# A perceiver layer on one core: the end of the second attention, with the last projections, the row norms and TensorE's filler matmuls rearranged

## The chip, the cores and the metric

The kernel runs on one core of a Trainium2 chip. The metric is the device time of one execution in microseconds (us). The engines are TensorE (PE; its weight loads are PEld), VectorE (DVE), ScalarE (ACT), GpSimd (POOL) and SyncE (SP), which issues most DMAs. Each runs its own instruction list in order; they wait for each other by semaphores, so an instruction behind a waiting one waits too.

## The reference, cut to what matters

```python
x = x + cross_attention(layernorm(x), ctx_768, ...)   # 16 heads, 4096 keys for each of 4 batches
x = x + attention(layernorm(x), w_qkv, ..., w_out)    # window of 32 tokens on either side, 16 heads
x = x + experts(layernorm(x), Wr, br, W1, b1, W2, b2) # 16 banks, 2 picked for each token

def experts(t, ...):
    probs = softmax(t @ Wr + br)                      # the router
    topv, topi = top_k(probs, 2)
    ...                                               # gate-weighted sum of the picked banks
```

x is 4 batches of 256 tokens of 256 numbers, in fp32. The change touches the end of the second line and the beginning of the third.

## The kernel before, in words

The 1024 tokens are held as 8 tiles of 128 rows, two for each batch. The first attention takes the first 900 us or so. The second works in 16 pairs (`PAIRS`) of a batch and a group of four heads. For pair i TensorE computes masked scores for the row maxima (`max2`, L799 and L805), which VectorE reduces (L1564) and splits into three bf16 pieces; TensorE turns these (`neg2`, L814), ScalarE copies them out (L1347), TensorE computes the transposed scores with the maximum subtracted (`scores2`, L833, L839 and L846), ScalarE takes the exponential in two halves (L1340), and TensorE multiplies by the values (`weigh2`, L863). In its list the steps of neighbouring pairs are interleaved. ScalarE copies a pair's output to `o_raw2` (L1299).

Outputs of the first 14 pairs (`WIDE`) go through small DMAs (`close_up`, and `close_rest` on ScalarE's queue) that put heads side by side in `o_close2` and sums in `total2`. VectorE takes the reciprocal (`inverse_two`, L1589); GpSimd multiplies (L2165) and adds the value bias (L2167), in `norm_two(u)`, u from 0 to 6. Pairs 14 and 15, the second half of the last batch's heads, go another way: TensorE turns them to tokens (`turn_out`, L872), VectorE divides (`tokens`, L1596 and L1600), TensorE turns them back (`turn_back`, L879), and ScalarE adds the bias (`out_back`, L1369).

The output projection of batch 2 is `project_third(0)` and `(1)` (L897), that of batch 3 is `project_wide` (L915, the half from u = 6) and `project_turned` (L922, the half that was turned back). VectorE adds them to x (`add_third`, L1609; `add_last2`, L1631) and computes the third layer norm: statistics (L1460, L1463), an inverse square root by small steps (L1472 to L1490). Normalised rows `xn3` are made on three engines: tiles 0 to 3 on GpSimd (L2177), 4 and 5 on ScalarE (`rows3`, L1376), 6 and 7 on VectorE (`apply`, L1499). TensorE transposes them (`turn3(b)`, L1010), ScalarE copies them out (L1382), TensorE computes the router's logits (L1029, 16 columns wide), and VectorE picks two banks a token (`choose`). TensorE then counts the tokens of each bank (`counts`, L1085); VectorE makes from it the list of tokens of each expert tile, on which the gathers and the loads of weights depend. The expert stage follows until the end.

`keep_busy(n, bank)` (L1017) multiplies the bf16 identity by itself n times, into a PSUM bank that nothing reads at that time. The "constants" of the change are these.

The order of work is written out by hand: each engine's block is its list. GpSimd, ScalarE and VectorE take their parts in an order of their own that has to fit TensorE's.

Of the kernel before, what the change touches and what calls it, by code (L numbers as in the profile page):

```python
# [12 lines left out]
ACT = mybir.ActivationFunctionType  # L13
# [4 lines left out]
BATCH, SEQ, EMB = 4, 256, 256  # L18
# [245 lines left out]
def build(nc, a, out, scratch):  # L264
    ctx = ExitStack()
    with ctx:
# [295 lines left out]
        def _(e):  # L562
# [348 lines left out]
            def project_wide():  # L911

                e.wait_ge(pool_norm2, WIDE // 2)
# [4 lines left out]
            def project_turned():  # L918

                e.wait_ge(act_ocopy2, PAIRS + 1)  # L920
# [77 lines left out]
            def turn3(b):  # L998
# [4 lines left out]
                else:  # L1003
                    if b == 2:
                        e.wait_ge(act_rows, TT)
                    else:
                        e.wait_ge(dve_rows3, BT)
# [50 lines left out]
            project_third(0)  # L1058
# [3 lines left out]
            turn_out(PAIRS - 2)  # L1062
            project_third(1)
            weigh2(PAIRS - 1, 0)
            weigh2(PAIRS - 1, 1)
            turn_out(PAIRS - 1)
            project_wide()
            turn_back()
            project_turned()
            turn3(0)  # L1070
            turn3(1)
            logits(range(0, 2), 2)
            keep_busy(8, 5)
            turn3(2)
            turn3(3)
            keep_busy(6, 5)
            logits(range(2, 3), 3)
            logits(range(3, 4), 4)
# [142 lines left out]
        def _(e):  # L1221
# [142 lines left out]

            def out_back():
# [6 lines left out]
            def rows3():  # L1372

                e.wait_ge(dve_root3, 2)
                for i in upper[:BT]:
                    e.activation(xn3[:, i], x[:, i], ACT.Identity, scale=rstd[:, i:i + 1], bias=sq[:, i:i + 1]).then_inc(act_rows, 1)  # L1376
# [3 lines left out]
            def turned3(b):  # L1380
                e.wait_ge(pe_t3, b + 1)
# [32 lines left out]
            ocopy2(PAIRS - 1)  # L1414
            out_back()
            turned3(0)
            turned3(1)
            rows3()
            turned3(2)
            turned3(3)  # L1420
# [33 lines left out]
        def _(e):  # L1454
# [319 lines left out]
            add_third(0)  # L1774
            inverse_two(WIDE // 2 - 1)
            tokens(0)
            add_third(1)
            e.wait_ge(dve_third, BT)
            statistics(upper[:BT])
            tokens(1)  # L1780
# [5 lines left out]
            shifted = slice(upper[0], upper[BT])  # L1786
            e.scalar_tensor_tensor(sq[:, shifted], mv[:, shifted, 0], -1.0, rstd[:, shifted], ALU.mult, ALU.mult).then_inc(dve_root3, 1)
            apply(xn3, upper[BT:], dve_rows3)
# [211 lines left out]
        def _(e):  # L2000
# [160 lines left out]
            def norm_two(u):  # L2161
# [3 lines left out]
                e.tensor_tensor(o, o, inverse2, ALU.mult).then_inc(pool_omul2, 1)  # L2165
                e.wait_ge(pool_omul2, u + 1)
                e.tensor_scalar_add(o, o, bv2[:, u % KE:u % KE + 1]).then_inc(pool_norm2, 1)  # L2167

            for u in range(WIDE // 2):
# [4 lines left out]
                if u == KE * (BATCH - 1) - 2:  # L2174
                    e.wait_ge(dve_root3, 1)
                    for i in range(TT // 2):
# [55 lines left out]
        def _(e):  # L2232
# [141 lines left out]
            for part in range(2):  # L2374
# [3 lines left out]
                else:  # L2378
                    e.wait_ge(act_rows, TT)
                    e.wait_ge(dve_rows3, BT)  # L2380
# [130 lines left out]
```

## Time and profile before

| | us |
|---|---|
| median of 3 runs | 1181.17 |
| lowest and highest of them | 1180.66, 1182.34 |
| the profiled execution | 1179.86 |
| its span, first to last instruction | 1178.1 |
| pair 15's maximum pieces done on VectorE | 935.2 |
| the last x rows added (L1631) | 947.5 to 948.4 |
| counts of banks read by VectorE | 961.8 |
| first expert tile turned (L1131) | 983.0 |

Times within the span are counted from its first instruction. TensorE is busy in 98% of the span, and the granted clock is 0.987 of full speed on the mean: full speed is 2.4 GHz, and its other level is 1.2 GHz. The profiled execution is 1.31 us faster than the median of the others. The rest of this text is about some 30 us in the last fifth of the span, between 930 and 962 us.

### The profile page before, as it was taken

The numbers are of one execution on the slowest core, as the hardware profiler recorded it, in microseconds if no ns is written. First come the engines' busy times: TensorE is split into PE (matmuls) and PEld (weight loads), VectorE is DVE, ScalarE is ACT, GpSimd is POOL, SyncE is SP. The second block draws the span as 40 slices with busy tenths as digits, with TensorE's granted clock in tenths as the row PEclk, the third lists the DMA queues.
The fourth block names the chain that finished last, engine by engine and source line by source line (L and its number), as shares of the span: only waits on it lengthen the run. The fifth ranks groups of instructions, "written<-read, shape, count | busy, mean of one in ns | idle before, by whom it ended". The sixth has DMA issues, their size and how long they took to land.

```text
span 1178.1 us, 29516 instructions
## 1 busy us (share of the span) xinstructions
PE 1150.7 (98%) x12028; PEld 712.7 (60%) x12028; DVE 841.1 (71%) x1637; ACT 706.0 (60%) x897; POOL 362.5 (31%) x336
## 2 busy tenths in 40 slices
PE   8989999999999999999999999999999989999998
PEld 5455555566555566654556654444556578877777
DVE  5987899977899987789997789982365672333234
ACT  4447788877788877778887778886333310211120
POOL 3386663113631513534311240021211312222220
PEclk9999999999999999999999999999999988999999
DMA  7766766555575465656654445401310119999993
GB/s 241 116 153 184 181 136 151 124 123 129 128 181 127 102 139 140 153 123 131 152 123 97 102 100 124 82 17 36 91 30 18 38 45 399 414 404 401 395 377 117
DMA packets 64654, 186.26 MB, mean 158 GB/s; under 512 B 20104, under 2 KB 29960, under 8 KB 56584
## 3 DMA queue, kind: packets, MB, share of 16 engines
q1 hardware_dynamic: 60260, 172.70, 53.3%
q0 software_dynamic: 2432, 7.11, 1.8%
q10 hardware_dynamic: 1828, 4.57, 1.1%
q8 instruction: 95, 1.56, 0.6%
q14 instruction: 39, 0.32, 0.1%
HBM read 137.60 MB, written 39.58 MB: 150 GB/s over the span
## 4 chain that ended last, share of the span: by engine, by line
PE 91%; DVE 3%; ACT 3%; issue 1%; POOL 1%; DMA 1%; SPq 0%; ACTq 0%; DVEq 0%; POOLq 0%
PE psum L750 22%; PE psum L732 17%; PE psum L702 11%; PE psum L1160 5%; PE psum L1188 5%; PE psum L600 5%; PE psum L616 4%; PE psum L805 2%; PE psum L1185 2%; PE psum L1154 2%; DVE part_max L1525 1%; ACT wts L1250 1%; PE psum L933 1%; PE psum L799 1%; PE psum L839 1%; PE psum L583 1%
## 5 line engine op out<-in xcount | busy, mean ns | idle before, releaser
L1535 DVE TENSOR_REDUCE part_max<-psum 128x1 f32<-128x512 f32 x952 | 599.6, 686 | 88.9 <-PE psum L702 87.1
L1250 ACT ACTIVATE wts<-psum 128x1024 f32<-128x1024 f32 x512 | 518.9, 1025 | 100.8 <-PE psum L732 100.0
L750 PE MATMUL psum<-wts,vals 128*17 128x256 f32 x4096 | 307.2, 384 | 0.5 <-ACT o_raw L1293 0.5
L732 PEld LDWEIGHTS psum<-queries,keys 51*128 51x128 f32 x2048 | 155.9, 185 | 187.3 <-issue 154.1
L732 PE MATMUL psum<-queries,keys 51*128 51x256 f32 x2048 | 255.2, 326 | 2.2 <-ACT queries L1282 0.2
L702 PE MATMUL psum<-keys,queries 51*128 51x512 f32 x1024 | 218.5, 409 | 4.2 <-DVE part_max L1525 2.5
L750 PEld LDWEIGHTS psum<-wts,vals 128*17 128x17 f32 x4096 | 74.9, 95 | 119.1 <-issue 93.4
L2013 POOL CAST key_high<-key_low 128x1024 fp32r<-128x1024 f32 x28 | 29.1, 1038 | 355.1 <-ACT key_low L1263 355.1
L702 PEld LDWEIGHTS psum<-keys,queries 51*128 51x128 f32 x1024 | 109.7, 185 | 20.1 <-DVE part_max L1525 10.7
L1441 ACT ACTIVATE hid<-psum,b1s 128x128 f32<-128x128 f32 (+1 forms) x124 | 31.7, 351 | 114.6 <-PE psum L1160 78.2
L2015 POOL TENSOR_TENSOR key_low<-key_low,key_high 128x1024 fp32r<-128x1024 f32 x28 | 66.6, 2379 | 2.3
L1160 PE MATMUL psum<-xTt,w1s 128*128 128x128 f32 x544 | 63.6, 275 | 0.4 <-issue 0.4
L1935 DVE TENSOR_SCALAR hid<-psum,b1s 128x128 f32<-128x128 f32 (+1 forms) x124 | 30.5, 314 | 45.5 <-PE psum L1160 42.4
L1160 PEld LDWEIGHTS psum<-xTt,w1s 128*128 128x128 f32 x544 | 62.2, 192 | 0.7 <-issue 0.6
L1188 PE MATMUL psum<-w2s,hid 128*128 128x256 f32 x272 | 62.1, 382 | 0.0
L2215 POOL DMA_INDIRECT rows_y<-yout,to_row x22 | 21.8, 990 | 129.6 <-DVE yout L1944 129.6
L1188 PEld LDWEIGHTS psum<-w2s,hid 128*128 128x128 f32 x272 | 50.4, 190 | 11.9 <-issue 5.7
L2028 POOL TENSOR_TENSOR ctx_lo<-ctx_in,ctx_hi 128x1536 fp32r<-128x1536 f32 x16 | 55.7, 3480 | 1.3
L1269 ACT ACTIVATE vals<-psum 128x512 f32<-128x512 f32 x64 | 38.3, 600 | 28.5 <-PE psum L616 16.4
L1263 ACT ACTIVATE key_low<-psum,bk_two 128x1024 f32<-128x1024 f32 x28 | 31.2, 1116 | 36.3 <-PE psum L600 36.3
L1564 DVE TENSOR_REDUCE neg_max<-psum 128x4 f32<-128x640 f32 x32 | 26.4, 825 | 33.6 <-PE psum L805 33.6
L1944 DVE COPY yout<-psum 128x256 f32<-128x256 f32 x22 | 9.3, 425 | 56.7 <-PE psum L1188 39.3
(277 smaller groups left out, 1387.7 us busy)
## 6 DMA issues: line engine op xcount, KB each, us to landing
w1s<-in_W SPq DMA_DIRECT2D x31, 1024.0 KB
w2s<-in_W SPq DMA_DIRECT2D x31, 1024.0 KB
keys<-k_high SPq DMA_DIRECT2D x232, 128.0 KB, 4.1
keys<-k_low SPq DMA_DIRECT2D x116, 128.0 KB, 4.6
k_high<-key_high SPq DMA_DIRECT2D x28, 512.0 KB, 5.1
k_low<-key_low SPq DMA_DIRECT2D x28, 512.0 KB, 5.5
ctx_in<-in_ctxT SPq DMA_DIRECT2D x12, 768.0 KB, 7.6
ctx_in<-in_ctxT ACTq DMA_DIRECT2D x4, 768.0 KB, 12.4
```

The lines of the kernel that those rows point to most:

```text
L600: t = e.matmul(bank(first + odd), w[rows, r, hp * P:(hp + 1) * P], c[rows, p, r * CH:(r + 1) * CH], start=(r == 0 and n == 0), stop=(r == ...
L616: m = e.matmul(bank(first + odd)[:, 0:EMB], c[rows, p, at:at + P], w[rows, r], start=(r == 0 and n == 0), stop=(r == CB - 1 and n == 2))
L702: e.matmul(bank(LEAD_BANKS[m % 2] + i if m < LEAD else M_BANKS[(2 * m + i) % 3]), queries[g % 3][64 * i:64 * i + STK, hh, qt * P:(qt + 1) ...
L732: m = e.matmul(bank(S_BANKS[S_NO["s", n] % 2] + i)[:, hh * SEQ:(hh + 1) * SEQ], keys[64 * i:64 * i + STK, hh, c, at:at + P], queries[g % 3 ...
L750: i = e.matmul(bank(O_BANK)[32 * j:32 * j + VW, 0:SEQ], vals[:, t, h * VW:(h + 1) * VW], wts[n % NW][:, j * SEQ:(j + 1) * SEQ], start=(t = ...
L1160: i = e.matmul(dst[:, q * P:(q + 1) * P], w1s[w[0]][:, k, hc * P:(hc + 1) * P], xTt[j % 2][:, k], start=(k == 0), stop=(k == KE - 1))
L1188: i = e.matmul(dst, hid[j % 2][:, hc], w2s[w[0]][:, hc], start=(hc == 0), stop=(hc == HC - 1))
L1250: i = e.activation(wts[n % NW], s_bank(job, 2), ACT.Exp, scale=QSCALE)
L1269: i = e.activation(vals_of[:, t:last + 1:CH // P, :, 0:HD], s_bank(job, 2).rearrange("p (t h w) -> p t h w", t=2, w=HD)[:, :, 0:HEADS], AC ...
L1535: e.reduce_max(part_max[g % 2][:, hq, c:c + 1], bank(M_BANKS[n % 3]), AX_X).then_inc(dve_max, 1)
L2015: e.tensor_tensor(key_low, key_f, key_high.bitcast(F32), ALU.subtract).then_inc(split_low, 1)
L2028: e.tensor_tensor(ctx_lo[:, p], ctx_in[:, p], ctx_hi[:, p].bitcast(F32), ALU.subtract).then_inc(pool_lo, 1)
```

## The change

- TensorE's `project_third(0)` stands behind `scores2(15)` and `turn_out(14)`, next to `project_third(1)`, and no longer ahead of `weigh2(14)`.
- `turn3(0)` and `turn3(1)` stand ahead of `turn_back`, and `project_wide` behind it.
- GpSimd normalises tiles 0 and 1 behind u = 4 and tiles 2 and 3 behind u = 5, where it did four behind u = 4. The last bias of u = 6 is added by ScalarE (`bias_wide`), and `project_wide` waits for that.
- VectorE takes its last `inverse_two` and `tokens(0)` ahead of `add_third(0)`, and `tokens(1)` ahead of the statistics of tiles 4 and 5.
- Of tiles 4 to 7, ScalarE normalises one (4) and VectorE three (6, 7, 5 in this order); batch 3 is turned and its logits are computed ahead of batch 2.
- Six filler matmuls are added ahead of `turn_out(15)`, and the eight behind the first logits are 26.

```diff
@@ def project_wide
-                e.wait_ge(pool_norm2, WIDE // 2)
+                e.wait_ge(act_ocopy2, PAIRS + 1)
@@ def project_turned
-                e.wait_ge(act_ocopy2, PAIRS + 1)
+                e.wait_ge(act_ocopy2, PAIRS + 2)
@@ def turn3
                     if b == 2:
-                        e.wait_ge(act_rows, TT)
+                        e.wait_ge(act_rows, TT - 1)
+                        e.wait_ge(dve_rows3, BT + 1)
@@ TensorE's list
             neg2(PAIRS - 1)
-            project_third(0)
             weigh2(PAIRS - 2, 0)
             weigh2(PAIRS - 2, 1)
             scores2(PAIRS - 1)
             turn_out(PAIRS - 2)
+            project_third(0)
             project_third(1)
             weigh2(PAIRS - 1, 0)
             weigh2(PAIRS - 1, 1)
+            keep_busy(6, L3_BANKS[1])
             turn_out(PAIRS - 1)
-            project_wide()
-            turn_back()
-            project_turned()
             turn3(0)
             turn3(1)
+            turn_back()
+            project_wide()
+            project_turned()
             logits(range(0, 2), 2)
-            keep_busy(8, 5)
+            keep_busy(26, T3_BANKS[1])
+            turn3(3)
             turn3(2)
-            turn3(3)
-            keep_busy(6, 5)
-            logits(range(2, 3), 3)
-            logits(range(3, 4), 4)
+            keep_busy(6, T3_BANKS[0])
+            logits(range(3, 4), 3)
+            logits(range(2, 3), 4)
@@ ScalarE
+            def bias_wide():
+
+                o = o_close2[(BATCH - 1) % 2][:, 0]
+                e.wait_ge(pool_omul2, WIDE // 2)
+                e.activation(o, o, ACT.Identity, bias=bv2[:, 0:1]).then_inc(act_ocopy2, 1)
+
@@ def rows3, now row3
-                for i in upper[:BT]:
-                    e.activation(xn3[:, i], x[:, i], ACT.Identity, scale=rstd[:, i:i + 1], bias=sq[:, i:i + 1]).then_inc(act_rows, 1)
+                i = upper[0]
+                e.activation(xn3[:, i], x[:, i], ACT.Identity, scale=rstd[:, i:i + 1], bias=sq[:, i:i + 1]).then_inc(act_rows, 1)
@@ ScalarE's list
             ocopy2(PAIRS - 1)
+            bias_wide()
+            turned3(0, 1)
             out_back()
-            turned3(0)
-            turned3(1)
-            rows3()
-            turned3(2)
-            turned3(3)
+            turned3(1, 2)
+            row3()
+            turned3(3, 3)
+            turned3(2, 4)
@@ VectorE's list
-            add_third(0)
             inverse_two(WIDE // 2 - 1)
             tokens(0)
+            add_third(0)
             add_third(1)
+            tokens(1)
             e.wait_ge(dve_third, BT)
             statistics(upper[:BT])
-            tokens(1)
             add_last2()
...
-            shifted = slice(upper[0], upper[BT])
+            shifted = slice(upper[0], upper[1])
...
-            apply(xn3, upper[BT:], dve_rows3)
+            apply(xn3, (upper[BT], upper[BT + 1], upper[1]), dve_rows3)
@@ GpSimd, norm_two and behind it
+                if u == WIDE // 2 - 1:
+                    return
...
-                if u == KE * (BATCH - 1) - 2:
+                if u in (KE * (BATCH - 1) - 2, KE * (BATCH - 1) - 1):
                     e.wait_ge(dve_root3, 1)
-                    for i in range(TT // 2):
+                    half = (u - KE * (BATCH - 1) + 2) * BT
+                    for i in range(half, half + BT):
@@ SyncE, store of the second half of xn3
-                    e.wait_ge(act_rows, TT)
-                    e.wait_ge(dve_rows3, BT)
+                    e.wait_ge(act_rows, TT - BT + 1)
+                    e.wait_ge(dve_rows3, BT + 1)
```

TensorE's list from the last pair's scores on (a line of before with -, of after with +; L1017 before and L1018 after are the filler matmuls; `o_close2_0_164` holds batch 2, `o_close2_1_165` batch 3, `wT0_150` to `wT3_153` the weights of pairs 14 and 15; the lines of after lie up to nine further down):

```order
 L846 MATMUL psum<-neg_rows2_0_148,ones2_141 128x160 x8
 L814 MATMUL psum<-identb_51,neg_parts2_1_147 128x128 x2
-L897 MATMUL psum<-wo2_143,o_close2_0_164 128x256 x2
 L863 MATMUL psum<-wT0_150,vals2_137 17x160 x4
 L863 MATMUL psum<-wT1_151,vals2_137 17x64 x4
```

and further down, from the turning of pair 14's output:

```order
 L872 MATMUL psum<-identf_50,o_raw2_0_154 128x128 x2
-L897 MATMUL psum<-wo2_143,o_close2_0_164 128x256 x2
+L897 MATMUL psum<-wo2_143,o_close2_0_164 128x256 x4
 L863 MATMUL psum<-wT2_152,vals2_137 17x160 x4
 L863 MATMUL psum<-wT3_153,vals2_137 17x64 x4
 L863 MATMUL psum<-wT3_153,vals2_137 17x96 x4
+L1018 MATMUL psum<-identb_51 128x128 x6
 L872 MATMUL psum<-identf_50,o_raw2_2_156 128x128 x2
+L1011 MATMUL psum<-identf_50,xn3_101 128x128 x8
+L879 MATMUL psum<-identf_50,by_tok_157 128x128 x2
 L915 MATMUL psum<-wo2_143,o_close2_1_165 128x256 x2
-L879 MATMUL psum<-identf_50,by_tok_157 128x128 x2
```

The first two matmuls of batch 2's projection have gone from ahead of pair 14's weighing to the place of the other two, behind the turning of pair 14's output. Eight transposes of normalised rows now stand ahead of the turning back, and `project_wide` behind it.

On GpSimd, around the two norms of batch 2's second half (`o_close_0_164` is batch 2, `xn_101` the normalised rows), before:

```order
L2177 TENSOR_SCALAR xn_101<-x,mv,rstd 128x256 [waits dve_root3]
L2177 TENSOR_SCALAR xn_101<-x,mv,rstd 128x256 x3
L2165 TENSOR_TENSOR o_close_0_164<-o_close_0_164,inverse_168 128x256 [waits dve_rec2]
L2167 TENSOR_SCALAR o_close_0_164<-o_close_0_164,bv_134 128x256 [waits pool_omul2]
L2165 TENSOR_TENSOR o_close_1_165<-o_close_1_165,inverse_168 128x256 [waits dve_rec2]
L2167 TENSOR_SCALAR o_close_1_165<-o_close_1_165,bv_134 128x256 [waits pool_omul2]
```

and after:

```order
L2189 TENSOR_SCALAR xn_101<-x,mv,rstd 128x256 [waits dve_root3]
L2189 TENSOR_SCALAR xn_101<-x,mv,rstd 128x256
L2174 TENSOR_TENSOR o_close_0_164<-o_close_0_164,inverse_168 128x256 [waits dve_rec2]
L2178 TENSOR_SCALAR o_close_0_164<-o_close_0_164,bv_134 128x256 [waits pool_omul2]
L2189 TENSOR_SCALAR xn_101<-x,mv,rstd 128x256 [waits dve_root3]
L2189 TENSOR_SCALAR xn_101<-x,mv,rstd 128x256
L2174 TENSOR_TENSOR o_close_1_165<-o_close_1_165,inverse_168 128x256 [waits dve_rec2]
```

Two of the four tiles have moved behind batch 2's last norm, and the last bias is gone from this engine.

## Rows read from the trace of the kernel before

**Rows 1.** The page: span, and TensorE's share of it.
```profile
span 1178.1 us, 29516 instructions
PE 1150.7 (98%) x12028; PEld 712.7 (60%) x12028; DVE 841.1 (71%) x1637; ACT 706.0 (60%) x897; POOL 362.5 (31%) x336
```

**Rows 2.** Windows of 2 us: length, busy us of engines, PEclk, DMA share, GB/s.
```profile
936.00:938.00 2.00, 0.83 (x4) 0.68 (x4) 0.00 (x0) 0.39 (x2) 1.01 (x2) 1.00 0.64 262
938.00:940.00 2.00, 2.00 (x29) 1.00 (x28) 1.54 (x2) 0.38 (x1) 0.00 (x0) 0.53 0.00 0
...
950.00:952.00 2.00, 1.84 (x21) 1.67 (x20) 1.76 (x10) 0.49 (x1) 0.00 (x0) 0.94 0.00 0
952.00:954.00 2.00, 1.34 (x7) 1.35 (x8) 1.79 (x16) 0.80 (x3) 0.00 (x0) 0.50 0.29 119
```

**Rows 3.** Timeline: start, length, engine, line, count, [idle before <-releaser]; pair 15's scores.
```profile
930.53 4.86 POOL L2177 TENSOR_SCALAR xn<-x,mv,rstd 128x256 f32<-128x256 f32 x4 [0.72 <-DVE rstd L1490]
...
933.16 0.72 PE L833 MATMUL psum<-wmaskb,identb 128*128 128x320 bf16 x4
...
933.81 0.82 PE L839 MATMUL psum<-q,k 32*128 32x160 f32 x16
...
934.81 1.30 ACT L1340 ACTIVATE wT<-psum 128x640 f32<-128x640 f32 x2 [2.67 <-PE psum L846]
...
935.36 0.72 POOL L2165 TENSOR_TENSOR o_close<-o_close,inverse 128x256 f32<-128x256 f32 x1
...
937.17 1.18 PE L897 MATMUL psum<-wo,o_close 128*128 128x256 f32 x4 [1.64 <-POOL o_close L2167]
...
938.28 1.27 PE L863 MATMUL psum<-wT,vals 128*17 128x160 f32 x24
...
938.80 1.74 DVE L1589 RECIPROCAL inverse<-total 128x256 f32<-128x256 f32 x1
...
939.48 1.25 PE L833 MATMUL psum<-wmaskb,identb 128*128 128x320 bf16 x4
...
940.66 1.23 PE L839 MATMUL psum<-q,k 32*128 32x160 f32 x16
```

**Rows 4.** Timeline from the last projections to the router's second logits.
```profile
942.23 1.03 PE L897 MATMUL psum<-wo,o_close 128*128 128x256 f32 x4
...
943.19 0.74 PE L863 MATMUL psum<-wT,vals 128*17 128x160 f32 x24
...
944.43 0.44 PE L872 MATMUL psum<-identf,o_raw 128*128 128x128 f32 x2 [0.51 <-ACT o_raw L1299]
...
946.69 1.13 PE L922 MATMUL psum<-wo,o_close 128*128 128x256 f32 x4 [0.56 <-ACT o_close L1369]
...
947.50 0.86 DVE L1631 TENSOR_TENSOR x<-psum,x 128x256 f32<-128x256 f32 x2 [1.86 <-PE psum L922]
947.66 1.04 PE L1010 MATMUL psum<-identf,xn 128*128 128x128 f32 x8
...
949.43 1.96 PE L1029 MATMUL psum<-wr,xT 128*128 128x16 f32 x16 [0.74 <-ACT xT L1382]
...
951.39 0.73 DVE L1499 TENSOR_SCALAR xn<-x,mv,rstd 128x256 f32<-128x256 f32 x2
951.51 1.09 ACT L1376 ACTIVATE xn<-x,sq,rstd 128x256 f32<-128x256 f32 x2 [2.13 <-DVE sq L1787]
...
952.65 1.97 PE L1010 MATMUL psum<-identf,xn 128*128 128x128 f32 x8 [0.81 <-ACT xn L1376]
...
955.05 3.54 PE L1029 MATMUL psum<-wr,xT 128*128 128x16 f32 x16
```

**Rows 5.** Timeline of the count of picked banks.
```profile
958.54 3.15 PE L1017 MATMUL psum<-identb 128*128 128x128 bf16 x28
...
960.92 0.23 DVE L1741 TENSOR_TENSOR both<-hots 128x64 bf16<-128x64 f32 x1
...
962.09 2.39 PE L1017 MATMUL psum<-identb 128*128 128x128 bf16 x40
```

More of the change, by code:

```diff
@@ L1370, in out_back, with row3, turned3 @@
                              bias=bv2[:, 1:2]).then_inc(act_ocopy2, 1)
-            def rows3():
+            def row3():
+                i = upper[0]
                 e.wait_ge(dve_root3, 2)
-                for i in upper[:BT]:
-                    e.activation(xn3[:, i], x[:, i], ACT.Identity, scale=rstd[:, i:i + 1], bias=sq[:, i:i + 1]).then_inc(act_rows, 1)
+                e.activation(xn3[:, i], x[:, i], ACT.Identity, scale=rstd[:, i:i + 1], bias=sq[:, i:i + 1]).then_inc(act_rows, 1)
             upper = range(TT // 2, TT)
-            def turned3(b):
-                e.wait_ge(pe_t3, b + 1)
+            def turned3(b, n):
+                e.wait_ge(pe_t3, n)
                 e.activation(xT3[b].rearrange("p k t -> p (k t)"), bank(T3_BANKS[b]), ACT.Copy).then_inc(act_t3, 1)
```

## The prediction

> **What bounds the kernel now.** The first view is the page: TensorE is busy in 98% of a span of 1178.1 us [rows 1]. A share of busy time does not tell whether a stretch is dense, so the second view is the windows: TensorE's count and time in each 2 us, and the clock that it was granted [rows 2]. The third is the timeline between 930 and 962 us [rows 3, 4, 5]. Three things are to be seen.
>
> First, a wait. Pair 14's weights were ready at 934.81 + 1.30 = 936.11, but TensorE's list had batch 2's first projection ahead of weighing them. That projection waited 1.64 us for GpSimd, whose norm began at 935.36 only, behind four normalised tiles of 4.86 us from 930.53 [rows 3]. Second, the clock. In the window with the wait, TensorE worked 0.83 of 2 us, and in the next one its clock stood at 0.53 of full, which is the 1.2 GHz level nearly throughout [rows 2]. The same instructions show the price: 1.25 us against 0.72 for the mask, 1.23 against 0.82 for the scores, 1.27 against 0.74 for the weighing [rows 3, 4]. Third, from 947.5 on a chain goes through VectorE (adds, statistics, inverse root), then the rows, eight transposes, the second logits, `choose` and the counts. Around 951.8 the clock falls again, after a window in which TensorE was busy 1.84 of 2 us, and the transposes take 1.97 us against 1.04, the logits 3.54 against 1.96, the 28 fillers 3.15 where 40 take 2.39 later [rows 2, 4, 5]. All that the experts wait for hangs on this chain.
>
> **The change part by part.** Times in the new order are estimates from the rows' starts and lengths.
>
> *Front.* The second half of pair 14's weighing starts at 936.16 and ends near 936.7. Pair 15's scores take 1.65 us (933.16 to 934.81, where the exponential begins), so they end at 938.3. In before they end near 942.05 (940.66 + 1.23, and the last of the subtraction). That is 3.7 us: 1.64 wait, 1.18 projection, 1.47 slow clock (0.53 + 0.41 + 0.53), less 0.6 now waited for the exponential.
>
> Is the projection's input there at 938.7, when the list comes to it? GpSimd now does two tiles (2.43 us, half of 4.86) from 930.53 to 933.0; the reciprocal of u = 5 ended at 933.3; multiplication and bias take 937.12 - 935.36 = 1.8 us: ready at 935.1. Hidden, with 3.5 us to spare. Tiles 2 and 3 end at 937.6 and are turned after 942: hidden. The store of these rows leaves 2.2 us later and is read by gathers 35 us on: nothing.
>
> What comes back: turning pair 14 (0.4, as pair 15's 0.44 [rows 4]), batch 2's two projections (0.9 each, 942.23 to 943.19 from start to start, where only one stood here), pair 15's weighing (0.74). Its end is 941.2, against 943.9: 2.7 us are left. Six fillers at 0.06 (2.39/40 [rows 5]) take 0.36 us inside the 0.51 that TensorE waited for ScalarE's copy: free. Pair 15 is turned by 942.1.
>
> *Middle.* From the end of the turning (944.87) to `project_turned` (946.69) lie 1.8 us in before: the division on VectorE, the turning back (0.4) and ScalarE's copy (0.5, as a tile of rows at 1.09/2), so about 0.8 for the division with its hand-overs [rows 4]. It ends at 942.8, but the turning back now stands behind eight transposes of 1.04 us, so it starts at 943.1: 0.3 us given away. It ends at 943.5, ScalarE's copy at 944.05, under `project_wide` (0.9, until 944.4). In before `project_turned` began at 946.69; now at 944.4. It is 2.3 us earlier, and so are the adds to x (947.50) and VectorE's chain. The statistics of batch 2 stand between: the same kind with the inverse root took 3.0 us (948.36 to 951.39), so alone they take at most half and fit between 942.8 and 945.2. ScalarE's new bias (nearest row 0.55) has from 941.6 to 943.5. `project_wide` waits for it: the reciprocal for it began at 938.80 in before, behind an add to x, so its small DMAs had landed by then; even at 938.8 reciprocal, product and bias are 1.74 + 0.75 + 0.5 = 3.0 us and end at 941.9, so nothing waits. From below this could be earlier than 938.8; it would gain nothing.
>
> *Row norms.* The rows began at 951.39 on VectorE, and the transposes at 952.65, when ScalarE's second tile was done: 1.26 us. Now VectorE's first two tiles are done after 0.73 us and start four transposes; its third ends after 1.10, ScalarE's one after 0.7, both before these transposes end. 0.45 us less.
>
> *Sum with the second fall of the clock as it was:* 2.3 + 0.45 = 2.75 us.
>
> *The second pause.* First logits end near 947.2, and 26 fillers at 0.06 last until 948.75; rows come at 949.9. In before the pause was 0.8 us after eight fillers. Cost at full clock: none. At half clock a filler takes 0.1125 (3.15/28), so 26 take 2.9 us; this is used in the rivals. What they may bring is a held clock: 0.93 on the transposes, 0.27 on six fillers, 1.58 on the logits (3.54 - 1.96), and of the 28 fillers, which now end the wait for the counts (958.54 + 3.15 = 961.69, while VectorE's `both` was ready at 961.15), 0.5: 3.3 us at most, from none. I take the low end. The row nearest is the window before the fall at 951.8: busy with 16-column matmuls and eight fillers, and it fell. In the new order the narrow logits, an idle us and narrow logits again still stand on both sides of the fillers, which thicken a part of it only.
>
> The Trainium skill (TensorE: Matmul & The Clock Gate, "HAM oscillation") puts the loss of the clock down to long idle gaps between groups of matmuls. By that rule this trace should not have lost it around 951.8, where TensorE had been busy 1.84 of 2 us; it did, so the measured row decides here. By the rule the new order would keep the full clock and come out at the time of the first rival below.
>
> **Own time and the median.** The profiled execution took 1179.86, 1.76 over its span; the median is 1181.17. Less 2.75 these are 1177.1 and 1178.4. The expert stage starts with the list that this chain makes, its loads of weights too, so all of it shifts; I forecast 1178.4 us against the median.
>
> **The rivals.**
> *Held clock* (22%): the 3.3 us above come on top: 6.0 us less, 1175.1. For it: 28 fillers at half clock brought it back at 962 [rows 5]. Against it: narrow logits on both sides. A part of it, for instance only the last logits at full clock, lies between.
> *The front saves less* (20%): the slow spell at 938 to 941.5 is in this execution, and nothing shows that it is in those of the median. Without it 1.47 us of the 2.75 were never lost there: 1.3 us less, 1179.9, which is within 0.2% of before.
> *Half clock through the fillers* (6%), the slower side: between 934.8 and 936.2 TensorE still waits for pair 15's last maxima and for the exponential, and if the clock falls at about 941 all the same, the new denser stretch pays the 1.5 us, the first logits pay 1.58, and 26 fillers last 2.9 instead of 1.55. `project_turned` begins at 945.9, logits end at 950.3, fillers at 953.2, against 952.65 for the transposes of before: +0.6 us, 1181.8, and 1182.5 if the weighing pays too. It decides from the point where these three exceed the 2.75 us gained.
> *The change does not do what it says* (2%): the DMAs or the turned projections take a new wait somewhere and the counts come when they came, 1181.2.
>
> **How the numbers follow.** The forecast itself has 50%, with its own range 1177.4 to 1179.4. A difference under 0.2% (2.4 us) can't be told from none here; the forecast of 2.75 is close to it, and I give 29 of its 50 to faster and 21 to the same. Held clock gives 22 to faster, the smaller front 19 to the same and 1 to faster, the slower case 3 to slower and 3 to the same, the last 1 to the same and 1 to slower. Faster 0.52, same 0.44, slower 0.04. The range runs from a partly held clock, 1175.6, to the smaller front and some scatter of the median, 1180.8.
>
> **What would show it.** In the trace after: pair 14's weighing straight behind the exponential, without a wait for GpSimd; pair 15's scores over by 938.3, and at 0.72 and 0.82 us for mask and scores; x added from 945.2; the first four transposes of the last batches at 949.9; the 26 fillers at 1.55 us. The clock between 949 and 957 tells the forecast from the held clock: transposes at 0.5 us for four, logits at 1.0 for eight. Wrong would be a fall before 945, a turning back that waits for VectorE, or a `project_wide` that waits for ScalarE's bias.

## The result, and the profile after

| | before | after |
|---|---|---|
| median, of 8 runs each on one chip | 1181.85 | 1173.72 |
| lowest and highest | 1180.54, 1182.78 | 1172.78, 1178.00 |
| the profiled execution | 1179.86 | 1173.59 |
| its span | 1178.1 | 1171.8 |
| mean granted clock in it | 0.987 | 0.994 |

The medians differ by 8.1 us, and their quotient is 0.9931. The ratio given with the runs is 0.9945, with a 95% interval of 0.9925 to 0.9965, which is 4 to 9 us: the changed kernel is faster, by less certain an amount than the medians alone suggest. The forecast was 1178.4, with a range down to 1175.6, so it was wrong. What came is the first rival, the held clock (1175.1), with a little more gained in order. The range had left that rival's own time out, although it had a chance of 22%.

The page of the profile after, against [rows 1]: TensorE has 24 more instructions and is busy 5.8 us less.

```profile
span 1171.8 us, 29565 instructions
PE 1144.9 (98%) x12052; PEld 709.0 (61%) x12052; DVE 841.8 (72%) x1638; ACT 705.4 (60%) x897; POOL 361.7 (31%) x335
```

The windows of 2 us after: length, busy us (count) of TensorE, its weight loads, VectorE, ScalarE and GpSimd, the granted clock, then the DMAs. The clock stands at 1.00 where [rows 2] have 0.53, 0.94 and 0.50, although TensorE is idle for 0.6 us in two windows.

```profile
936.00:938.00 2.00, 2.00 (x38) 1.48 (x32) 1.37 (x1) 0.70 (x2) 1.63 (x2) 1.00 0.03 14
938.00:940.00 2.00, 2.00 (x21) 1.48 (x23) 1.14 (x5) 0.98 (x2) 0.36 (x4) 1.00 0.60 248
...
946.00:948.00 2.00, 1.37 (x25) 1.19 (x22) 1.69 (x12) 0.09 (x1) 0.00 (x0) 1.00 0.00 0
948.00:950.00 2.00, 1.43 (x15) 1.33 (x15) 1.90 (x14) 1.24 (x3) 0.00 (x0) 1.00 0.14 59
950.00:952.00 2.00, 2.00 (x24) 2.00 (x25) 1.22 (x8) 0.35 (x1) 0.00 (x0) 1.00 0.50 203
952.00:954.00 2.00, 1.55 (x28) 1.37 (x25) 1.79 (x16) 0.00 (x0) 0.00 (x0) 1.00 0.03 8
```

TensorE's timeline after, in place of [rows 3] and [rows 4]: start, length, engine, line, tiles, count, and in brackets the wait ahead of it.

```profile
935.12 0.97 PE L863 MATMUL psum<-wT,vals 128*17 128x160 f32 x24
936.03 0.72 PE L833 MATMUL psum<-wmaskb,identb 128*128 128x320 bf16 x4
936.68 0.83 PE L839 MATMUL psum<-q,k 32*128 32x160 f32 x16
...
937.85 1.89 PE L897 MATMUL psum<-wo,o_close 128*128 128x256 f32 x8
939.67 0.74 PE L863 MATMUL psum<-wT,vals 128*17 128x160 f32 x24
940.35 0.51 PE L1018 MATMUL psum<-identb 128*128 128x128 bf16 x6
...
942.07 0.42 PE L879 MATMUL psum<-identf,by_tok 128*128 128x128 f32 x2
942.33 1.03 PE L915 MATMUL psum<-wo,o_close 128*128 128x256 f32 x4
943.19 1.03 PE L922 MATMUL psum<-wo,o_close 128*128 128x256 f32 x4
944.05 1.85 PE L1030 MATMUL psum<-wr,xT 128*128 128x16 f32 x16
945.76 1.61 PE L1018 MATMUL psum<-identb 128*128 128x128 bf16 x26
948.57 1.09 PE L1011 MATMUL psum<-identf,xn 128*128 128x128 f32 x8 [1.21 <-DVE xn L1508]
949.50 0.50 PE L1018 MATMUL psum<-identb 128*128 128x128 bf16 x6
949.91 1.96 PE L1030 MATMUL psum<-wr,xT 128*128 128x16 f32 x16
951.72 0.24 PE L1087 MATMUL psum<-both,ones 128*128 128x16 bf16 x4
951.82 1.72 PE L1018 MATMUL psum<-identb 128*128 128x128 bf16 x28
```

The mask and scores of pair 15 take 0.72 and 0.83 us, not 1.25 and 1.23. The wait of 1.64 us for GpSimd is gone. The second transposes take 1.09 us against 1.97, the second logits 1.96 against 3.54, the 28 fillers 1.72 against 3.15. And there is still a wait of 1.21 us behind the 26 fillers, in which the clock does not fall.

VectorE and ScalarE on the same chain:

```profile
943.89 0.86 DVE L1640 TENSOR_TENSOR x<-psum,x 128x256 f32<-128x256 f32 x2 [0.69 <-PE psum L922]
947.79 1.05 DVE L1508 TENSOR_SCALAR xn<-x,mv,rstd 128x256 f32<-128x256 f32 x3
947.91 0.60 ACT L1384 ACTIVATE xn<-x,sq,rstd 128x256 f32<-128x256 f32 x1 [4.42 <-DVE sq L1796]
```

To compare kernels I cut this chain at five instructions: VectorE's last maximum pieces of pair 15; the first of the last x rows added (L1640 after, L1631 before); the first of the last rows normalised; their first transpose; the table `filled`, made from the counts. What lies ahead of the first does not count, and that matters, since the stretch began between 932.9 and 942.1 us in the kernels profiled below.

| profiled | pieces to x | x to rows | to transposes | to `filled` | sum |
|---|---|---|---|---|---|
| before | 12.50 | 3.89 | 1.27 | 9.16 | 26.83 |
| after | 9.44 | 3.90 | 0.78 | 6.20 | 20.32 |
| difference | 3.06 | 0 | 0.49 | 2.96 | 6.51 |

From `filled` to the first expert turn it takes 21.26 us after and 21.20 before. Then 0.7 is given back at the first split expert tile, one whose rows belong to two banks. TensorE idles 0.97 us ahead of it against 0.25 in the kernel before. Its list waits there for the tile's weights; the profile names no releaser, so that they are the cause is an inference:

```profile
989.31 3.23 PE L1156 MATMUL psum<-w1s,xTt 128*64 128x512 f32 x14 [0.97 <-issue]
```

A difference of 0.53 us already stands ahead of the change: the mask of pair 14 (L833) begins at 932.62 and not 933.16. So the spans should differ by 0.53 + 6.51 - 0.06 - 0.72 = 6.26, and they differ by 6.3. The 0.72 belongs to this execution and not to the change: in two more profiles of the same kernel (after_again and after_third below) the same wait is 0.21 and 0.42. From `filled` to the last instruction it takes 217.0 us in this profile, 216.3 and 216.4 in those two, and 216.2 in the kernel before.

### The profile page after: what moved, and what is told of

It reads as the page before. It is cut to its first block, busy times and chain, and to the rows that moved or that the text cites. A ratio compares the mean times of both kernels' runs of the same rounds, so it can differ in the third digit from the quotient of the medians.

```text
span 1171.8 us, 29565 instructions
## 1 busy us (share of the span) xinstructions
PE 1144.9 (98%) x12052; PEld 709.0 (61%) x12052; DVE 841.8 (72%) x1638; ACT 705.4 (60%) x897; POOL 361.7 (31%) x335
## 4 chain that ended last, share of the span: by engine, by line
PE 89%; DVE 4%; ACT 3%; DMA 2%; issue 1%; SPq 1%; ACTq 0%; POOL 0%; DVEq 0%; POOLq 0%
PE psum L750 22%; PE psum L732 17%; PE psum L702 11%; PE psum L1162 5%; PE psum L1190 5%; PE psum L600 5%; PE psum L616 4%; PE psum L1187 2%; PE psum L1156 2%; PE psum L805 2%; DVE part_max L1534 1%; ACT wts L1252 1%; PE psum L933 1%; PE psum L799 1%; DMA ctx_in<-in_ctxT 1%
## 5 line engine op out<-in xcount | busy, mean ns | idle before, releaser
L750 PEld LDWEIGHTS psum<-wts,vals 128*17 128x17 f32 x4096 | 74.9, 95 | 119.1 <-issue 92.4
L1944 DVE TENSOR_SCALAR hid<-psum,b1s 128x128 f32<-128x128 f32 (+1 forms) x124 | 30.5, 313 | 45.5 <-PE psum L1162 42.4
```

The source lines that it names most:

```text
L750: i = e.matmul(bank(O_BANK)[32 * j:32 * j + VW, 0:SEQ], vals[:, t, h * VW:(h + 1) * VW], wts[n % NW][:, j * SEQ:(j + 1) * SEQ], start=(t = ...
```

## The experiments

They were timed in four groups, each on one chip and beside the kernel before, with one profile a run. The kernel before had medians of 1180.82 us beside few_fillers, before_26, front_alone and front_undone, 1180.58 beside middle_undone, norms_undone, no_six and after_again, 1180.39 beside few_fillers_2, fillers_17, fill_mid and fill_both, and 1181.09 beside after_third, no_six_2, no_six_3 and norms_undone_2. The sums stand for the stretch above. "low clock" is where the granted clock fell between 930 and 980 us, with the length of the spell. A ratio below 1 is faster than before.

| run | pieces to x | x to rows | to transposes | to `filled` | sum | low clock from (for) |
|---|---|---|---|---|---|---|
| before | 12.50 | 3.89 | 1.27 | 9.16 | 26.83 | 938.1 (3.4), 951.8 (10.2), 972.2 (10.2) |
| after | 9.44 | 3.90 | 0.78 | 6.20 | 20.32 | 965.5 (10.2) |
| before_26 | 11.00 | 3.89 | 1.30 | 6.17 | 22.36 | 965.8 (3.4), 972.6 (6.8) |
| few_fillers | 9.44 | 3.89 | 0.79 | 9.17 | 23.28 | 948.7 (10.2), 969.2 (10.2) |
| few_fillers_2 | 9.43 | 3.89 | 0.78 | 9.11 | 23.22 | 950.1 (10.2), 970.6 (6.8) |
| fillers_17 | 9.43 | 3.89 | 0.79 | 9.16 | 23.28 | 949.7 (10.2), 970.2 (10.2) |
| front_alone | 9.52 | 3.90 | 1.26 | 9.16 | 23.85 | 947.3 (10.2), 967.8 (10.2) |
| front_undone | 12.43 | 3.89 | 0.79 | 6.21 | 23.31 | 940.2 (3.4), 970.9 (10.2) |
| middle_undone | 9.58 | 3.89 | 1.30 | 6.15 | 20.92 | 967.9 (3.4), 974.7 (6.8) |
| norms_undone | 9.43 | 3.89 | 1.26 | 6.20 | 20.79 | 964.8 (3.4), 971.6 (6.8) |
| norms_undone_2 | 9.44 | 3.89 | 1.26 | 6.21 | 20.80 | 969.4 (10.2) |
| no_six, and twice more | 9.44 | 3.89 | 0.79 | 6.20 | 20.32 | 968.3, 969.4, 968.2 (10.2 each) |
| after_again | 9.44 | 3.90 | 0.79 | 6.20 | 20.33 | 964.1 (10.2) |
| after_third | 9.43 | 3.89 | 0.79 | 6.20 | 20.32 | 965.6 (10.2) |
| fill_mid | 9.43 | 3.89 | 0.79 | 6.20 | 20.31 | 966.5 (10.2) |
| fill_both | 9.44 | 3.89 | 0.78 | 6.21 | 20.32 | 958.8, 969.0, 975.9 (3.4 each) |

### The fillers alone

```diff
 few_fillers, few_fillers_2 (fillers_17: 17), on the changed kernel
-            keep_busy(26, T3_BANKS[1])
+            keep_busy(8, T3_BANKS[1])
 before_26, on the kernel before
-            keep_busy(8, 5)
+            keep_busy(26, 5)
```

> The kernel after, with 8 filler matmuls behind the first logits in place of 26. Theory A (the 26 fillers hold TensorE's clock through the row norms' pause): the clock falls near 946 to 952 in most executions, the eight transposes and the second logits go back to some 1.9 and 3.5 us, and the time rises by 2.5 to 3.3 us over the kernel after, to about 1176.5. Theory B (it is the denser order in front of them that holds it): the clock stays and the time is that of after within 0.5 us, 1173.7. Rival C (the clock is a matter of chance from run to run): the runs spread over both times in both kernels.

> The kernel before, with 26 fillers in place of 8 behind the first logits and nothing else. Theory A: the clock holds, transposes 1.0 and second logits 2.0 us, 2.5 to 3.3 us faster than before, about 1179. Theory B: no change, or up to 0.2 us slower where the fillers end behind the rows, 1181.9.

> The changed kernel with 8 filler matmuls behind the first logits where it has 26, run a second time, since a fall of the clock could be chance in one profiled execution. Theory A (the 18 fillers hold the clock): the clock falls again between 947 and 953, and from the last maximum pieces of pair 15 to `filled` it is 23.0 to 23.5 us. Theory C (falls come by chance): it may as well be 20.3, as in all executions profiled with 26. Median 1176 to 1178.5 by A.

> The changed kernel with 17 filler matmuls behind the first logits where it has 26 and the kernel before 8. With 26 the time from the last maximum pieces of pair 15 to `filled` was 20.3 us and with 8 it was 23.3, with the clock low from 948.7. Theory A (the fillers hold the clock): 17 last 1.05 us and leave a wait of about 1.75 us with nothing in it; either they are enough, 20.3 us and no fall before 964, or they are not, 23.3 with a fall between 948 and 953; I expect them to be enough with 0.5. Theory B (the denser order holds it and the fall with 8 was chance): 20.3.

Measured: few_fillers 1177.77 us, ratio 0.9983 (0.9963 to 1.0002); the second time 1177.47, 0.9981 (0.9965 to 0.9997); fillers_17 1176.75, 0.9969 (0.9949 to 0.9989); before_26 1181.04, 1.002 (0.9999 to 1.004).

TensorE in few_fillers, and its windows:

```profile
946.65 0.61 PE L1018 MATMUL psum<-identb 128*128 128x128 bf16 x8
949.46 1.97 PE L1011 MATMUL psum<-identf,xn 128*128 128x128 f32 x8 [2.21 <-DVE xn L1508]
951.22 0.85 PE L1018 MATMUL psum<-identb 128*128 128x128 bf16 x6
951.86 3.54 PE L1030 MATMUL psum<-wr,xT 128*128 128x16 f32 x16
```

```profile
946.00:948.00 2.00, 1.25 (x16) 1.08 (x15) 1.74 (x11) 0.00 (x0) 0.00 (x0) 1.00 0.00 0
948.00:950.00 2.00, 0.54 (x3) 0.54 (x4) 1.85 (x10) 0.60 (x1) 0.00 (x0) 0.68 0.00 0
950.00:952.00 2.00, 2.00 (x14) 1.94 (x13) 1.79 (x16) 1.13 (x2) 0.00 (x0) 0.50 0.64 262
```

With 8 fillers the wait for the rows is 2.21 us, the clock falls in it, and everything behind is as slow as in the kernel before: 9.17 against 9.16. Only this part of the table moves. With 17 fillers it moves as little:

```profile
947.89 1.11 PE L1018 MATMUL psum<-identb 128*128 128x128 bf16 x17
950.71 1.97 PE L1011 MATMUL psum<-identf,xn 128*128 128x128 f32 x8 [1.71 <-DVE xn L1508]
```

I had given 17 an even chance. The step lies between 17 and 26, and it is a step: 9.17, 9.16, 6.20. In all five profiles with 8 or 17 fillers (the kernel before and front_alone among them) the clock falls here, and in all thirteen with 26 it holds. The timed executions point the same way: of the 34 of few_fillers, its repeat and fillers_17 none had a mean clock over 0.991, while 17 of 24 of the changed kernel had 0.993 or 0.994. But 17 of 110 of the kernel before, with its 8 fillers, had that too. Either 8 fillers do not lose the clock here every time, or these 17 were spared another spell; no profile caught one of them. In before_26 18 more fillers bring the old order 2.99 in this part. There the pause was 0.8 us after eight fillers, and now it is filled whole:

```profile
952.90 1.61 PE L1017 MATMUL psum<-identb 128*128 128x128 bf16 x26
954.35 1.06 PE L1010 MATMUL psum<-identf,xn 128*128 128x128 f32 x8
955.25 0.50 PE L1017 MATMUL psum<-identb 128*128 128x128 bf16 x6
```

So the fillers hold the clock in either order; a denser order without them does not (few_fillers). The median of before_26 does not show the 4.5 us that its profile gains in the stretch. Its stretch begins 3.2 us later (938.16 against 934.99), behind low clock at 30.5, 74.9 and 129.5 us (the kernel before has only 74.5 of these), far ahead of anything that the experiment touches. Only one of its 12 executions has a clock of 0.993. So the whole time of this run can't be used for the price of the fillers; the stretch can.

### The front alone, and undone

```diff
 front_undone, on the changed kernel (front_alone is the same the other way, on the kernel before)
+            project_third(0)
             weigh2(PAIRS - 2, 0)
             weigh2(PAIRS - 2, 1)
             scores2(PAIRS - 1)
             turn_out(PAIRS - 2)
-            project_third(0)
...
+            add_third(0)
             inverse_two(WIDE // 2 - 1)
             tokens(0)
-            add_third(0)
...
-                if u in (KE * (BATCH - 1) - 2, KE * (BATCH - 1) - 1):
+                if u == KE * (BATCH - 1) - 2:
...
-                    half = (u - KE * (BATCH - 1) + 2) * BT
-                    for i in range(half, half + BT):
+                    for i in range(TT // 2):
```

> The kernel before, with the third batch's first projection behind the last scores, GpSimd's four tiles in two parts and VectorE's last reciprocal ahead of the add; the middle, the row norms and the fillers as before. The steps of the forecast give 3.7 us for the scores and 2.7 us at pair 15's output, and the chain behind it shifts by that: 2.7 us faster, 1179.1. Rival (the slow spell at 938 to 941 was not in every execution of before): 1.2 us faster, 1180.6.

> The kernel after, with that front put back as before (projection ahead of pair 14's weighing, four tiles in one part, the add ahead of the reciprocal). If front and fillers add up, it loses what front_alone gains: 2.7 us slower than after if the slow spell comes back, 1176.4, or 1.2 us, 1174.9, if it does not. If the clock then falls ahead of the row norms too, more: up to 1179.

Measured: front_alone 1178.07, 0.9991 (0.9973 to 1.0009); front_undone 1179.04, 0.9991 (0.9963 to 1.0018), with executions from 1173.39 to 1188.86. Neither median tells the front's worth; the stretch does. TensorE in front_undone, where the projection waits for GpSimd again:

```profile
938.81 1.13 PE L897 MATMUL psum<-wo,o_close 128*128 128x256 f32 x4 [1.63 <-POOL o_close L2178]
939.87 0.99 PE L863 MATMUL psum<-wT,vals 128*17 128x160 f32 x24
940.79 1.25 PE L833 MATMUL psum<-wmaskb,identb 128*128 128x320 bf16 x4
```

and in before_26, with the same wait:

```profile
940.33 1.13 PE L897 MATMUL psum<-wo,o_close 128*128 128x256 f32 x4 [1.63 <-POOL o_close L2167]
941.39 0.74 PE L863 MATMUL psum<-wT,vals 128*17 128x160 f32 x24
942.07 0.72 PE L833 MATMUL psum<-wmaskb,identb 128*128 128x320 bf16 x4
```

The front brings 12.50 - 9.52 = 2.98 us alone and 12.43 - 9.44 = 2.99 in the full change. Of this 1.50 are the low clock (12.50 against 11.00 in before_26). That spell is not certain: behind one same wait the clock fell in before and in front_undone, 0.9 and 1.4 us after the wait had ended, and did not fall in before_26. The order itself is worth 1.5, the clock another 1.5 in those executions that lose it. The new order takes away the wait, so nothing is lost there in any of its profiles.

### The middle, the norms and the six fillers

```diff
 middle_undone (ScalarE's turned3(0, 1) back behind out_back too)
-            turn3(0)
-            turn3(1)
-            turn_back()
             project_wide()
+            turn_back()
             project_turned()
+            turn3(0)
+            turn3(1)
 norms_undone, norms_undone_2: row3, apply, and the order of batches 2 and 3 as before
-                i = upper[0]
-                e.activation(xn3[:, i], x[:, i], ...)
+                for i in upper[:BT]:
+                    e.activation(xn3[:, i], x[:, i], ...)
...
-            apply(xn3, (upper[BT], upper[BT + 1], upper[1]), dve_rows3)
+            apply(xn3, upper[BT:], dve_rows3)
 no_six, no_six_2, no_six_3
-            keep_busy(6, L3_BANKS[1])
 after_again, after_third: no edit
```

> The kernel after with the middle in the order of before: project_wide, the turning back and project_turned ahead of the eight transposes of batches 0 and 1. By the forecast's step the turning back starts 0.3 us earlier, under the projection's cover, but project_wide stands in VectorE's wait and not in ScalarE's, and the copies of the transposes end later: the add to x comes 0.2 us earlier to 0.2 later, the time is within 0.3 us of after. Rival: with the transposes behind the turned projection the first logits wait for ScalarE (0.7 us) and a gap in a stretch of narrow matmuls costs the clock: 3 us slower, 1177.

> The kernel after with the row norms of tiles 4 to 7 divided as before (two on ScalarE, two on VectorE, batch 2 turned first). The forecast's step: the transposes start 0.45 us later, so 0.45 us slower than after where the clock holds, 1174.2. Rival: the longer pause lets the clock fall, and it is 3 us slower, 1177.

> The kernel after without the six fillers ahead of pair 15's turning. They stand in a wait of 0.5 us that is there anyway, so theory A expects the same time, 1173.7 to 1174.5. Rival: they too keep the clock, and without them executions with a fall near 942 to 945 appear, 1.5 us slower on the median.

> The kernel after, unchanged, once more beside the kernel before. The eight runs of after had a median of 1173.7 and the eight of before 1181.9, but 35 runs of before have since spread from 1174 to 1186 with the granted clock. Theory A (the change holds the clock in the stretch 945 to 962 us in most executions): most runs have a clock of 0.993 or 0.994 and 1173 to 1174.5 us, a few 0.988 to 0.991 and 1176 to 1178; median 1174. Rival C (the eight runs were a lucky draw): the same two groups as before, median 1177 or over.

Measured: middle_undone 1177.37, 0.9987 (0.9967 to 1.0006); norms_undone 1177.87, 0.9977 (0.9956 to 0.9999); no_six 1175.73, 0.9962 (0.9943 to 0.9982); after_again 1172.31, 0.9943 (0.9922 to 0.9963).

In the stretch all four are plain. The norms are worth 0.47, at the place foretold (1.26 against 0.79 until the first transpose). The six fillers are worth nothing, 20.32 with and without. The middle is worth 0.14 until x, and 0.5 more at the transposes; 0.3 at most had been expected in all, and it is 0.60. At the transposes the 26 fillers are then in the way: eight transposes come ahead of the logits, so the fillers begin later and end 0.5 after the rows are ready, with no wait behind them:

```profile
953.61 1.96 PE L1030 MATMUL psum<-wr,xT 128*128 128x16 f32 x16 [0.74 <-ACT xT L1390]
955.42 1.61 PE L1018 MATMUL psum<-identb 128*128 128x128 bf16 x26
956.87 1.04 PE L1011 MATMUL psum<-identf,xn 128*128 128x128 f32 x8
```

But the medians of the three variants are 3 to 6 us above the 1172.31 of the changed kernel beside them, which the stretch does not explain. So no_six, norms_undone and the changed kernel have further runs; middle_undone has none.

> The changed kernel once more. If its executions hold the clock up to the expert lists as a property of its order, 8 or more of 10 have a mean clock of 0.993 or above, as 15 of 18 did so far, with a median of 1172 to 1174. If that was chance of these two loadings, about as few as of its variants (3 of 12), with a median of 1176 to 1178. From the last maximum pieces of pair 15 to `filled`: 20.3 us in either case, in the execution profiled.

> The changed kernel without the six filler matmuls ahead of pair 15's turning, a second time. If the six hold the clock in some executions, only 2 or 3 of 12 are again at 0.993 or above, the median is 1175 to 1176, and the profile may show a fall between 940 and 950 with 22 to 23.5 us from the last maximum pieces to `filled`. If they do nothing, the distribution is that of the changed kernel of the same call, and 20.3 us stand there.

> The same kernel a third time, for a third profile: as the one before. A fall between 940 and 950 in one of the two would show that the six fillers matter; none in both, with a lower mean clock all the same, would put the falls outside this stretch.

> The changed kernel with the norms of tiles 4 to 7 divided as in the kernel before (two on ScalarE, two on VectorE, batch 2 turned first), a second time. The wait behind the 26 fillers is 1.68 us there, not 1.21. If that longer wait loses the clock in some executions, a fall stands at about 950 with 23.5 to 24 us from the last maximum pieces to `filled`, and few executions are at 0.993 or above; if not, 20.8 us as in the first profile, and the lower clock of its executions comes from elsewhere.

Measured: after_third 1173.59, 0.9942 (0.9923 to 0.9961); no_six_2 1175.21, 0.9949 (0.9929 to 0.9969); no_six_3 1173.98, 0.9942 (0.9923 to 0.9962); norms_undone_2 1175.12, 0.9956 (0.9935 to 0.9976).

The stretch repeats within 0.01 us each time. The medians don't: no_six had 1175.73, 1175.21 and 1173.98, norms_undone 1177.87 and 1175.12. In no_six_2 and norms_undone_2 low clock stands at 30.8, 75.1 and 129.8 us, in norms_undone at 838.5 for 13.7 us. The stretches of these three begin 4 to 5 us later than in the changed kernel's profile. In middle_undone low clock stands at 841.6 for 13.7 us, and its stretch begins 7.6 us later. After_third had 2 of 6 executions at 0.993 or more, where 15 of 18 were there before, so the high share was partly luck. The lower clock of the variants comes from spells upstream of the change, in the profiles that show it; for the executions that were not profiled this remains an inference.

### Two more places to fill

```diff
 fill_mid, in the first loop over pairs of the second attention
+                if i == 1:
+                    e.wait_ge(act_s, len(S_JOBS))
+                    keep_busy(10, 0)
 fill_both: the same, and ahead of the second matmuls of the expert lists
-                keep_busy(30, 5)
+                keep_busy(56, 5)
```

> The changed kernel with ten filler matmuls in TensorE's wait of 0.71 us at 839, at the change-over between the attentions. Theory A: no fall of the clock between 836 and 852 in the profile, and nearly all executions at a mean clock of 0.993 or more, median 1172 to 1173. Theory C: some executions still at 0.988 to 0.991 (1176 to 1178), as of variants whose code up to there is that of the changed kernel. From the last maximum pieces of pair 15 to `filled`: 20.3 us by both.

> The changed kernel with two more sets of filler matmuls: ten (a multiply of 128x128 each) in TensorE's wait for VectorE's maxima of the second attention's second pair (0.71 us at 839 in the trace after), and 56 where 30 stand ahead of the second matmul group of the expert lists, behind the wait for which the clock fell in the trace after at 965.5. If fillers hold the clock wherever they fill a wait (theory A), neither fall is seen: the second matmul group ahead of `from_row` takes 1.1 us and not 1.8, the first expert turn comes 0.7 earlier behind `filled`, and the median is about 1171.5 against 1172.3 to 1173.7 of the changed kernel, with few executions above 1174. If falls come by chance from run to run (theory C), the spread stays (1172 to 1178) and a fall stands somewhere near 965 all the same. If 26 more fillers are longer than the wait they fill, the first turn comes later by up to 1 us. From the last maximum pieces of pair 15 to `filled`: 20.3 us by both.

Measured: fill_mid 1174.69, 0.9949 (0.9931 to 0.9967); fill_both 1174.96, 0.9961 (0.9941 to 0.9981). Neither beats the changed kernel. In fill_mid the clock holds at 839, but it held there in the profile of after too, so this tells little; and where nearly all executions had been expected at a mean clock of 0.993 or more, 3 of 6 were. In fill_both the expectation failed too: the clock fell at 958.8, ahead of the longer set, in waits that did not lose it in any other profile with 26 fillers. It stayed low until 962.2, through the first 1.8 us of the 56 fillers.

```profile
958.57 1.94 PE L1113 MATMUL psum<-b,gT 32*128 32x512 f32 x8
960.43 4.12 PE L1018 MATMUL psum<-identb 128*128 128x128 bf16 x56
964.36 1.93 PE L1118 MATMUL psum<-at_tile,at_row 128*128 128x24 f32 x16
...
976.02 0.69 PE L1136 MATMUL psum<-identf,xin 128*128 128x128 f32 x2 [2.15 <-DMA xin<-rows_x,from_row]
976.50 5.06 PE L1165 MATMUL psum<-xTt,w1s 128*128 128x128 f32 x32
```

These matmuls began 10.4 us behind `filled` (964.36 - 953.96) and not 9.1 (963.89 - 954.78), but the wait and the low clock that the changed kernel has between and behind them were gone. So the list that the gathers of rows read (`from_row`) was ready 12.81 us behind `filled` and 12.82 in the changed kernel: nothing won, nothing lost. What followed lost. TensorE waited 2.15 us for the second tile's rows, the clock fell at 969.0 and 975.9, and the first tile's first product took 5.06 us where the changed kernel takes 3.81. From `filled` to the last instruction it is 218.8 us, against 216.3 to 217.0 in the changed kernel's three profiles. All ten timed executions had a mean clock of 0.994 to 0.997, as high as the changed kernel's best or higher, and still a median of 1174.96: a higher mean clock, bought with fillers, was no shorter time.

## Why the prediction was wrong

*The failed step* is one sentence: "I take the low end", 0 of a possible 3.3 us for a held clock behind the first logits. It measured 2.96: 0.88 on the transposes, 0.35 on the six fillers, 1.58 on the logits, and 0.15 at the last fillers, where the bound had 0.5. The upper bound was good and the choice of its low end was not. I argued from the window before the fall at 951.8, busy 1.84 of 2 us with narrow matmuls on either side of a few fillers, and from the narrow logits that stay on both sides. Few_fillers and fillers_17 show that the narrow logits do stay and the clock does fall with them alone; 26 fillers of 0.06 us are what turns it. The upper end was also the nearer row in kind: [rows 5] have 28 fillers in a row just ahead of the clock's return at 962.0, and I named them only for the rival.

The Trainium skill (TensorE: Matmul & The Clock Gate, "HAM oscillation") lays lost clock to idle gaps between groups of matmuls. By it the rival's time followed, and the time came out near that. That does not bear the rule out. This case's trace agrees with it only in that the wait of 1.21 us in the new order does not lose the clock. The fall at 951.8 of the kernel before came behind 1.84 of 2 us of work, and in the same new order few_fillers and fillers_17 lost the clock in waits of 2.21 and 1.71 us.

*The front and the middle, until x:* forecast 2.3, measured 3.06. The three terms of the front held: the wait is gone, the projection moved, mask and scores run at 0.72 and 0.83, and front_alone has 2.98 of it. What I took off again was too much. I had added whole lengths of rows, while the next instruction starts before a matmul's length is over: from start to start the eight transposes take 0.88 (941.19 to 942.07) and not 1.04, the turning back 0.26 and not 0.4. Less the 0.53 that lies upstream, the turning back began 0.5 sooner than forecast and `project_turned` 0.7. That is a fifth of the miss; 2.96 of 3.76 are the clock.

*The rival of the smaller front* named a real thing: the low clock at 938 is there in some executions and not in others. It priced 1.3; 1.50 was measured. It did not reduce the gain of the median, which was 8.1; how many of the executions that were not profiled lose the clock there stays open.

*Middle and project_wide:* ScalarE's bias ended at 941.26 and cost nothing; both projections ran without a wait. *Row norms:* forecast 0.45, measured 0.47 to 0.49. *Six fillers:* forecast free, measured free. *The half clock through the fillers* was seen in no profile of the new order. *Expert stage:* I shifted all of it, and that held. The 0.7 given back at the first split tile in the first profile is scatter: the same kernel's other two profiles have that wait at 0.21 and 0.42, the kernel before at 0.25.

*The median:* the profile moved by 6.3 us and the median by 8.1. The 1.8 between them lie in the kernel before, whose profiled execution was 2.0 faster than the median of 1181.85. Most likely they come from how often the clock falls, within the stretch and elsewhere; no profile shows it. Of 110 timed executions of the kernel before, 17 had a mean clock of 0.993 or 0.994, at about 1175 us; of 24 of the changed kernel, 17, at about 1173. So at like mean clock the order gains some 2 us, and the stretch says the same: 22.36 - 20.32 = 2.04 between before_26 and after. The rest of the 8 is then clock held. Of it the profiles show 1.50 + 2.96 = 4.5 us in the stretch; the other 1.6 are not shown.

## What to carry to other kernels

A filler set in a pause is not priced by what it costs alone: work out both ends, what each matmul behind it takes at the full clock and at half, and ask what in the trace brought a lost clock back. Here 18 more fillers of 0.06 us in a wait that was there anyway were worth 3 us in the stretch, more than all the reordering around them at full clock (2.04), and 9 more were worth nothing. Each such place has to be tried by itself: the longer set at the expert lists in fill_both gained nothing. When medians of variants scatter more than the edit can explain, compare the edited stretch between two fixed instructions of the profile. It repeated to 0.01 us in three kernels, where the medians moved by up to 2.7, and to 0.06 in a fourth. That holds only if the same spells of low clock lie in it: the one at 938 moved it by 1.5 with the order unchanged.

## What the runs showed of the hardware

- The same wait may or may not be followed by a fall of the clock. 1.63 us at the projection: lost in before and front_undone, held in before_26. A wait of 0.71 us at about 838, at code that the change does not touch: in before and after_third the clock fell at 839.1 and 839.3, 1.0 and 1.2 us after the wait had ended, and in after and after_again it held. (The second attention begins there, at 829.8 in the kernel before, and not near 900.) The mask of four matmuls behind it, in after_third and then in after_again:

```profile
839.02 0.68 PE L805 MATMUL psum<-k,q 32*128 32x160 f32 x4
839.64 1.25 PE L833 MATMUL psum<-wmaskb,identb 128*128 128x320 bf16 x4
```

```profile
838.93 0.72 PE L833 MATMUL psum<-wmaskb,identb 128*128 128x320 bf16 x4
```

- The spells of low clock in these profiles lasted 3.4, 6.8, 10.2 or 13.7 us. A fall behind the first logits lasted 10.2 in all five profiles that have one, with transposes and 16-column logits at the lower level in it; the one at the projection, with wide scores behind it, 3.4.
- Wherever the clock fell near 950 it fell again at the expert lists, at 967.8 to 972.2. Where it held near 950 it fell at the lists too, at 959 to 971. The 26 fillers do not remove that one.
